# Moving VectorE's side operations ahead of a PSUM drain in the neighbourhood stage of a fused attention kernel

## The reference, cut to what matters

```
# 1. neighbourhood attention (4 heads of 16, window 7 x 7) with an MLP
qkv  = layernorm(x) @ qkv_w + qkv_b
attn = softmax(q . k over the 7 x 7 window + relative position bias)
x    = x + (attn @ v) @ proj_w + proj_b
x    = x + gelu(layernorm(x) @ fc1_w + fc1_b) @ fc2_w + fc2_b
# 2. global attention (8 heads of 64) over all 1024 tokens of an image
t    = t + attention(layernorm(t), Wq, Wk, Wv) @ Wu + bu
# 3. a routed scan of 33 blocks: the operation is chosen from the state's first row,
#    and each block attends and/or feeds the state forward, or leaves it alone
t    = t + routed(layernorm(t), ...)
```

## Time and profile before

| | |
|---|---|
| time, median of 3 runs | 614.19 us (614.12 to 620.15) |
| the profiled execution's own time | 615.03 us |
| its span (first to last instruction) | 613.2 us |
| busy share of the span | PE 89%, DVE 66%, ACT 52%, POOL 8% |
| neighbourhood stage | from about 24 to 153 us of the span |
| mean granted TensorE clock over the span | 0.945 |

### The profile page before, as it was taken

How to read it: one execution, slowest core, us unless ns; L and a number is a source line. 1 busy time by engine, 2 the same in 40 slices (tenths; PEclk the granted TensorE clock), 3 DMA queues, 4 the chain that set the end, 5 groups by cost and what they waited for, 6 DMA issues and landing times.

```text
span 613.2 us, 11018 instructions
## 1 busy us (share of the span) xinstructions
PE 548.1 (89%) x4271; PEld 296.8 (48%) x4272; DVE 405.8 (66%) x740; ACT 316.9 (52%) x584; POOL 51.1 (8%) x106
## 2 busy tenths in 40 slices
PE   6999998999699989999999999999999933799962
PEld 5554654555244435454555554445555410266621
DVE  5555547455886745886877677776663357798763
ACT  2645445834155574556655556556566433465440
POOL 6030233212110000000000010000000000000000
PEclk9999999977889999999999999999999958899977
DMA  5000000000000000000000000000000000000001
GB/s 114 1 2 1 2 3 1 1 1 2 1 1 1 1 1 2 2 0 1 2 1 0 2 2 1 1 10 1 1 1 0 1 4 6 10 1 1 2 0 34
DMA packets 9514, 3.33 MB, mean 5 GB/s; under 512 B 8820, under 2 KB 9079, under 8 KB 9463
## 3 DMA queue, kind: packets, MB, share of 16 engines
q1 hardware_dynamic: 8182, 2.61, 1.9%
q10 hardware_dynamic: 1281, 0.01, 0.1%
HBM read 2.09 MB, written 0.52 MB: 4 GB/s over the span
## 4 chain that ended last, share of the span: by engine, by line
PE 78%; DVE 9%; issue 7%; ACT 3%; POOL 1%; POOLq 0%; DVEq 0%; ACTq 0%
PE PS L766 18%; PE PS L789 17%; PE PS L750 8%; PE PS L671 4%; PE PS L685 4%; PE PS L698 3%; PE PS L522 2%; PE PS L712 2%; PE PS L730 2%; PE PS L494 2%; PE PS L506 2%; PE PS L805 2%; PE PS L994 2%; PE PS L568 2%; PE PS L586 1%
## 5 line engine op out<-in xcount | busy, mean ns | idle before, releaser
L1557 DVE TENSOR_REDUCE most<-PS 128x2 f32<-128x1024 f32 x128 | 156.3, 1223 | 71.9 <-PE PS L750 71.2
L1193 ACT ACTIVATE PT<-PS 128x512 f32<-128x512 f32 x256 | 138.8, 596 | 75.6 <-PE PS L766 75.2
L766 PE MATMUL PS<-qS,aS 128*64 128x512 f16 x1024 | 135.6, 383 | 2.0 <-ACT PT L1193 1.9
L789 PE MATMUL PS<-PT,V 128*64 128x512 f32 x512 | 132.8, 592 | 0.0
L766 PEld LDWEIGHTS PS<-qS,aS 128*64 128x64 f16 x1024 | 61.3, 111 | 62.1 <-issue 20.4
L750 PE MATMUL PS<-aS,qS 128*64 128x512 f16 x512 | 81.0, 391 | 4.4 <-DVE most L1557 4.0
L1149 ACT ACTIVATE prob<-sbias,negm 128x320 f32<-128x320 f32 (+1 forms) x64 | 34.3, 538 | 42.9 <-DVE negm L1603 42.6
L789 PEld LDWEIGHTS PS<-PT,V 128*64 128x64 f32 x512 | 40.0, 137 | 19.5 <-issue 0.8
L750 PEld LDWEIGHTS PS<-aS,qS 128*64 128x64 f16 x512 | 32.1, 111 | 30.3 <-DVE most L1557 8.4
L671 PE MATMUL PS<-ident 128*128 128x256 f16 x128 | 39.9, 312 | 6.3 <-DVE negm L1603 5.4
L1312 POOL TENSOR_TENSOR rstd<-var,minus_half 128x8 f32<-128x8 f32 (+1 forms) x9 | 13.5, 1504 | 355.4 <-DVE var L1420 355.4
(11 more groups left out here) (192 smaller groups left out, 670.4 us busy)
## 6 DMA issues: line engine op xcount, KB each, us to landing
xall<-in_x_dram SPq DMA_DIRECT2D x2, 256.0 KB, 4.4
out_dram<-x SPq DMA_DIRECT2D x4, 128.0 KB, 2.1
w<-in_L_attn_Wq_dram SPq DMA_DIRECT2D x2, 128.0 KB, 2.5
w<-in_L_attn_Wk_dram SPq DMA_DIRECT2D x2, 128.0 KB, 2.7
w<-in_L_attn_Wv_dram SPq DMA_DIRECT2D x2, 128.0 KB, 2.7
fc<-in_L_conv_fc_w_dram SPq DMA_DIRECT2D x2, 64.0 KB, 2.4
wu<-in_L_attn_Wu_dram SPq DMA_DIRECT2D x2, 64.0 KB, 2.4
w1s<-in_L_ffn_ffn_w_dram SPq DMA_DIRECT2D x2, 64.0 KB, 2.1
```

The lines of the kernel that those rows point to most:

```text
L766: mm = pe.matmul(PS[h0:h0 + C, lane, :], aS[:, k0 + h0:k0 + h0 + C], qS[:, part, lane, toks], start=(part == 0), stop=(part == 1))
L789: mm = pe.matmul(PS[cols, 6 + g % 2, :], V[:, img * NT + kt, cols], PT[:, g % 2, lane, kt, :], start=(kt == 0), stop=(kt == NT - 1))
L1193: act.activation(PT[:, g % 2, lane, phase, :], PS[:, lane, :], ACT.Exp).then_inc(c1["exped"], 1)
L1557: dve.tensor_reduce(most[:, g % 2, u // 2, u % 2, :], banks, AX.X, ALU.max, negate=True)\
```

## The change

In DVE's loop, the side operations of a step are moved to stand directly behind score+bias. The drain of the unit two back, `weigh_heads` and the calls of `drain_q(1)` and `drain_k(1)` come behind them. `drain_a`, the queries' pieces and `greatest` stay behind all of that. No operation, shape or table entry changes.

```
--- before
+++ after
@@ the vector engine's loop over steps, behind score+bias @@
-                u = i - 2
-                if 0 <= u < UN0 and u % 2 == 1:
-                    dve.wait_ge(c0["hi_turned"], u // 2 + 1)
-                    nat_drain(dve.tensor_copy, None, HI, u).then_inc(c0["hi_drained"], 1)
-                if i >= LAG_WEIGH and (i - LAG_WEIGH) % NH0 == 0:
-                    weigh_heads((i - LAG_WEIGH) // NH0)
-
                 if 0 <= i - LN1_STEP < LN:
                     moment(2, xall[:, tiles_of(1), :], i - LN1_STEP)
...
                 if i == at_step["x", 1][1]:
                     drain_x(1, "x", 0)
-                if i == at_step["q", 1][1]:
-                    drain_q(1)
-                if i == at_step["k", 1][1]:
-                    drain_k(1)
                 if i == at_step["v", 1][1]:
                     drain_v(1)
...
                 if i == LN3_STEP:
                     divide(4, twice=True)
+
+                u = i - 2
+                if 0 <= u < UN0 and u % 2 == 1:
+                    dve.wait_ge(c0["hi_turned"], u // 2 + 1)
+                    nat_drain(dve.tensor_copy, None, HI, u).then_inc(c0["hi_drained"], 1)
+                if i >= LAG_WEIGH and (i - LAG_WEIGH) % NH0 == 0:
+                    weigh_heads((i - LAG_WEIGH) // NH0)
+                if i == at_step["q", 1][1]:
+                    drain_q(1)
+                if i == at_step["k", 1][1]:
+                    drain_k(1)
                 if i == at_step["a", 0][1]:
                     drain_a(0)
```

## The result

| | before | changed |
|---|---|---|
| median | 614.82 us (20 runs, 612.01 to 621.23) | 625.28 us (20 runs, 616.28 to 635.53) |
| profiled execution, its own time | 615.03 us | 626.23 us |
| span | 613.2 us | 624.4 us |
| mean granted clock | 0.945 | 0.924 |

The ratio changed / before is 1.0092, with a 95% interval of [1.0052, 1.0133]. It compares only the executions of either kernel that lie within 1.5% of its fastest, which leaves out the upper half of the changed kernel's, although they are long through the very mechanism that the change sets off; the ratio of all medians is 1.017. By both the kernel became slower.

A forecast was written before the change was run, and what follows sets the result against it. PE was taken to bound the kernel (busy 89% of the span, 78% of the chain). Order +1.6 us and a clock fall of +6.0 us gave +7.6 us on 614.19, so 621.8 us, range 614.8 to 628.

The forecast's parts named there:

- step 25: DVE step with centre_weights twice: centring waits for PE's transposed weights, so the step ends 0.88 us later.
- step 53: DVE step with add_mlp: it starts as before, drain and weighing come behind it, so the end is 1.08 us later.
- step 41: DVE step with moment operations on data long in SBUF: they start 0.60 us earlier, net -0.36 us.
- step 39's wait for `attended`: In DVE's queue, now ahead of the drain of unit 37: takes 0.24 us of the 0.60 us gain.
- Sum of the order: Neighbourhood stage, reordered step ends without the clock: 0.88 + 1.08 - 0.36 = +1.6 us.
- Steps 3 and 5: A moment operation moves ahead of a drain, PE doesn't wait there: taken as 0, at most 0.6 us each.
- The clock at step 25: Likeliest case (0.55): PE's wait at 77.38 grows to 1.81 us and the clock falls; 621.8 us, 618.7 to 628.
- The price per us at 1.2 GHz: Loss per us at half clock: 0.42 if PE alone sets the pace, 0.29 if DVE becomes the floor.
- The length of the stretch: Half-clock time behind step 25: 17 us, costing 6.0 us; bounds 10 us and twice 17 us.
- the wait of 1.54 us at 103.33: PE's wait at step 41 before the change; the clock survived it, which spoke for the clock staying.
- The stretch near 130 us: 17 us at 1.2 GHz from 129.8, behind step 53's wait; its ending early or not occurring was a 0.04 rival, 609.8 us.
- Rival 1: At step 25 the longer wait is paid once and the clock stays: +1.6 us, 615.8 us, chance 0.36.

The follow-up runs named there:

- all but step 25: Changed kernel with the two centre_weights calls put back behind drain and weighing, all else reordered: 616.38 us, ratio 0.9989.
- fillers in step 25: Changed kernel with eight filler matmuls on PE at the start of step 26, in the 1.81 us wait: 617.38 us, ratio 1.0049.
- step 25 alone: Kernel before with only the four centring operations moved ahead of drain and weighing: 624.09 us, ratio 1.011.
- foreign delay: Kernel before in its own order, with one more VectorE product of about 0.9 us behind the centring of step 25: 624.02 us, ratio 1.0118.
- step 53 alone: Kernel before with only add_mlp(0) moved ahead of the drain: 616.5 us, ratio 1.0078.
- fillers in step 54: Kernel before with six filler matmuls on PE at the start of step 54 alone: 609.39 us, ratio 0.9896.
- step 41 alone: Kernel before with only the two moment operations of steps 40 to 42 moved ahead of the drain: 610.72 us, ratio 0.9912.

## Why the prediction was right, and where it was not

**The step ends.** Score+bias of the next unit came 0.88 us later at step 25 (it starts 5.13 us behind that of unit 25, where it was 4.25) and 1.08 to 1.09 later at step 53, and PE's waits grew to 1.81 and 1.98 us; forecast were 1.81 and 1.97. At step 41 the wait fell to 1.14 us in the two runs of the changed order whose clock was up there (all but step 25, and fillers in step 25), forecast was about 1.2: step 39's wait for `attended` took 0.20 of the 0.60, not 0.24. Sum of the order: 0.88 + 1.08 - 0.40 = 1.56 us, forecast 1.6. The reasoning that the drain has no deadline inside its step, so that only the last operation's end counts, holds: no row of the changed kernel has PE waiting for the late drain. Steps 3 and 5, taken as 0, gave 0.09 us: the filler at 36.19 us before stands at 36.10.

**The clock at step 25.** This was the likeliest case (0.55), and it happened. PE was busy 2.19 us in the slice with the wait, as reckoned from the earlier trace rows (4 less a wait of 1.81), and the clock fell right behind it. The runs with step 25 alone, with fillers and with a foreign delay show that PE's idle time there is the cause. That the busy share of a slice tells a fall beforehand is not shown: the slice from 100 with the 1.54 us wait has 2.46 busy us in the kernel before, where the clock stayed, and in the run with step 53 alone, where it fell. The rule of the Trainium skill (TensorE: Matmul & The Clock Gate, section "HAM oscillation — how this bites in real kernels"), by which the clock would have stayed, is not borne out: waits of 1.81, 1.54 and 0.89 us each stood ahead of a fall. The two levels of its section "What's actually happening" agree with every slice: 1.00, 0.50, or a mixture of the two.

**The price per us at 1.2 GHz.** The profiled execution has 11.6 us in the stage; less 1.56 for the order, 10.1 are left for the clock. The changed kernel spent 34 us more at 1.2 GHz behind 44 us (51 against 17); ahead of that it spent about 7 us less there (5.6 to 9.2, below). 10.1 / (34.1 - 7) = 0.37 per us (0.35 to 0.41), between the bounds of 0.29 and 0.42. The split is bookkeeping in one point: at step 41 the changed kernel gained no 0.40 us in this execution, as the stretch at half clock took up the whole wait there.

**The length of the stretch** is the term that was mis-sized. I took 17 us, from the one stretch of before in this stage, and 34 us as the upper bound (whose dearer price already gives 614.19 + 1.6 + 14 = 629.8, above the 628 at which the range ends). In the profiled execution it was 41 us, in the two others that show it 20 (step 25 alone) and 27 (the foreign delay). The 6.0 us that it gave were 10.1 in the profiled execution, and 10.46 - 1.56 = 8.9 by the medians. So the forecast of 621.8 lies 3.5 us under the median of 625.28; the range of 614.8 to 628 held it, but 7 of the 20 runs lie above 628. My upper bound rested on one row for a quantity that varies from one execution to the next. It is in part luck that the sum came no further off: in the profiled execution the stretch was 24 us longer than taken, but the clock rose some 7 us earlier and the stretch of step 53 was 7 us shorter, and the forecast's sum had neither.

**What the clock survived.** The sentence that the wait of 1.54 us at 103.33 cost no clock was true of that execution (and of the one with fillers in step 54), not of the kernel. With step 53 alone reordered the clock fell behind the same wait, and in 3 of the 5 profiled executions that have it; with it shortened the time fell by 3.9 us where the order explains 0.6. Here the prediction leaned on one execution. This understated the gain of step 41 by itself, in which I saw 0.36 us.

**The stretch near 130 us** I expected to stay, and took no change from it. In the changed kernel it stands at 143.7, behind the same step, and is 10 us long instead of 17. That gave back a part of what the stretch of step 25 took.

**The chances.** By the ratio 1.0092 the result is within 1%, at its upper edge, which had 0.50; by all medians it is 1.7% slower, which had 0.48. Rival 1 (the clock stays, 615.8) is seen too: 2 of the 20 runs, 616.28 and 616.73 us, have the granted clock of before (0.945 and 0.946), and they lie 1.5 to 1.9 us above the median of before.

## What to carry to other kernels

Cost an order change by when the last operation of a step ends, and look at what the engine on the path does in that time: an operation that waits for a late producer belongs behind work that is ready, not ahead of it. If TensorE is that engine, a wait of 0.9 to 2 us in such a stage has a second price, the chance of a stretch at half clock, here several times the wait itself. A few fillers in the wait can buy it back: six in one step made the kernel before 5 us faster. They don't secure the clock: in two filled kernels it still fell in the profiled execution, at places without fillers.

## What the runs showed of the hardware

**The first stretch at half clock is not in the clock column.** In the slices up to 44 us the kernel before has a granted clock of 1.00, but its fillers take 393 ns up to 43.6 us and 283 ns from 45.3 us on. The same in the changed kernel, only that there the step lies between 36.1 and 38.0 us. At the stretch that the column does show at 0.50, the fillers take 392 ns as well, so the column leaves out a first stretch at half clock. L671 of the kernel before (up to 44, then 45 to 129, then 129.6 to 147 us), and of the changed one (up to 37, then 38 to 75):

```profile
L671 PE MATMUL PS<-ident x21: 371/393/422, 24.6 to 43.6; 128*128 128x256 f16 x21
...
L671 PE MATMUL PS<-ident x88: 272/283/284, 45.3 to 128.0; 128*128 128x256 f16 x88
...
L671 PE MATMUL PS<-ident x14: 283/392/421, 129.5 to 146.7; 128*128 128x256 f16 x14
```

```profile
L671 PE MATMUL PS<-ident x15: 370/393/421, 24.6 to 36.1; 128*128 128x256 f16 x15
...
L671 PE MATMUL PS<-ident x38: 272/283/283, 38.0 to 72.9; 128*128 128x256 f16 x38
```

Up to there the two kernels differ in two moved operations (one each in steps 3 and 5), which brought PE 0.09 us. The order isn't needed for the difference: the run with step 41 alone has the instructions of the kernel before up to step 40, and its fillers are fast from 38.2 us on. These are its slow ones, and those of the run with the longer step 25, also identical up to there:

```profile
L671 PE MATMUL PS<-ident x15: 371/394/418, 24.6 to 36.2; 128*128 128x256 f16 x15
```

```profile
L672 PE MATMUL PS<-ident x22: 370/393/421, 24.6 to 46.2; 128*128 128x256 f16 x22
```

So the time at which the clock first rises differs between executions by itself, by 5.6 to 9.2 us between the two kernels and by at least 8 us (38.2 against 46.2) over all of these, and everything later meets the clock at another point. It fits the scatter of the kernel before (605.37 to 622.8 us over all sets), but no experiment held the first rise fixed, so that it causes the scatter is argued and not shown.

**Fillers cost nothing where PE waits:** eight of them take 0.87 us, 0.11 us each, and the wait behind them shrinks by the same amount.
